# Routed gate and up products with the rows stationary and the weights moving, their result turned by TensorE, and silu in place of tanh of the half

## What is computed

```python
topk_idx, tw = _route(x, router_w, bias)          # 4 of 16 experts for a row
h = jnp.einsum('td,edf->etf', x, gate_w)
u = jnp.einsum('td,edf->etf', x, up_w)
y = jnp.einsum('etf,efd->etd', jax.nn.silu(h) * u, down_w)
routed = jnp.einsum('etd,te->td', y, combine)
sh = jax.nn.silu(x @ sh_gate_w) * (x @ sh_up_w) @ sh_down_w
```

## Time and profile before

| | |
|---|---|
| median of 3 runs | 1787.53 us (1786.2 to 1792.46) |
| the profiled execution's own time | 1785.15 us |
| its span | 1783.4 us |
| mean granted TensorE clock | 0.898 |
| PE busy | 1371.1 us (77%), 11876 matmuls |
| PEld (weight loads) busy | 767.6 us (43%) |
| DVE busy | 1065.8 us (60%) |
| ACT (ScalarE) busy | 1005.3 us (56%) |
| POOL busy | 592.5 us (33%) |

### The profile page before, as it was taken

How to read it: one execution, slowest core, us unless ns; L and a number is a source line. 1 busy time by engine, 2 the same in 40 slices (tenths; PEclk the granted TensorE clock), 3 DMA queues, 4 the chain that set the end, 5 groups by cost and what they waited for, 6 DMA issues and landing times.

```text
span 1783.4 us, 34295 instructions
## 1 busy us (share of the span) xinstructions
PE 1371.1 (77%) x11876; PEld 767.6 (43%) x11876; DVE 1065.8 (60%) x2525; ACT 1005.3 (56%) x1690; POOL 592.5 (33%) x557
## 2 busy tenths in 40 slices
PE   5776476776579898987899989777977785798870
PEld 2211131233225653655356536443545553676650
DVE  7785436454746576477556764874568757234533
ACT  4899577765576698674766976655661121121110
POOL 2100111031533221326332113375535353724426
PEclk9767787898889999998999999988998887999995
DMA  6558400000122342343324323443437423545533
GB/s 191 164 177 197 105 1 24 1 24 13 50 75 66 96 120 54 103 112 107 107 78 111 104 60 96 107 123 117 113 106 202 136 78 94 139 95 142 143 93 118
DMA packets 217939, 180.26 MB, mean 101 GB/s; under 512 B 115467, under 2 KB 188851, under 8 KB 217779
## 3 DMA queue, kind: packets, MB, share of 16 engines
q1 hardware_dynamic: 205491, 144.49, 30.1%
q0 software_dynamic: 12288, 33.57, 6.1%
HBM read 86.25 MB, written 66.58 MB: 86 GB/s over the span
## 4 chain that ended last, share of the span: by engine, by line
PE 37%; ACT 21%; DVE 19%; issue 10%; POOL 7%; DMA 3%; another core or an unknown queue 1%; SPq 1%; POOLq 0%; DVEq 0%; ACTq 0%
ACT big L1131 17%; PE psF L912 8%; DMA big<-in_x 2%; PE psG L762 2%; PE psU L762 2%; PE psY L762 2%; PE psF L762 2%; DVE xc L1462 2%; PE psU L764 2%; PE psF L764 2%; PE psU L763 2%; PE psF L763 2%; POOL big L753 2%; PE psY L763 2%; PE psY L764 2%
## 5 line engine op out<-in xcount | busy, mean ns | idle before, releaser
L1131 ACT ACTIVATE big<-big,text_bias 128x512 f32<-128x512 f32 x1232 | 776.1, 711 | 148.2 <-PE psF L912 59.3
L912 PE MATMUL psF<-big,wslide 128*32 128x512 f32 x2464 | 395.8, 695 | 129.5 <-ACT big L1131 122.0
L698 POOL TENSOR_TENSOR hid_lo<-tile,hid_hi 128x512 f16<-128x512 f32 x128 | 151.0, 1179 | 567.2 <-ACT hid_hi L1146 567.0
L1146 ACT CAST hid_hi<-tile 128x512 f16<-128x512 f32 x128 | 78.4, 613 | 227.8 <-DVE tile L1512 195.4
L762 PE MATMUL psY<-big,hid_hi 128*128 128x256 f16 (+1 forms) x496 | 140.3, 283 | 78.5 <-issue 43.9
L912 PEld LDWEIGHTS psF<-big,wslide 128*32 128x32 f32 x2464 | 54.7, 115 | 290.1 <-ACT big L1131 251.9
L762 PE MATMUL psG<-xg,gate_hi 128*128 128x128 f16 x768 | 159.6, 227 | 11.3 <-issue 4.6
L745 POOL TENSOR_TENSOR work<-work 128x512 f16<-128x512 f32 (+1 forms) x80 | 92.8, 1162 | 219.2 <-DVE work L1636 218.7
L1508 DVE SCALAR_TENSOR_TENSOR tile<-tile,psG 128x512 f32<-128x512 f32 x128 | 87.4, 683 | 123.6 <-ACT tile L1159 108.2
L763 PE MATMUL psG<-xg,gate_hi 128*128 128x128 f16 x768 | 156.1, 222 | 1.4 <-issue 1.4
L764 PE MATMUL psG<-xg,gate_lo 128*128 128x128 f16 x768 | 156.0, 222 | 1.0 <-issue 1.0
(11 more groups left out here) (317 smaller groups left out, 2912.9 us busy)
## 6 DMA issues: line engine op xcount, KB each, us to landing
big<-down_split SPq DMA_DIRECT2D x138, 256.0 KB
y_rows<-tile SPq DMA_DIRECT2D x96, 256.0 KB
xs_rows<-peakT SPq DMA_DIRECT2D x2, 6144.0 KB, 47.6
big<-in_x SPq DMA_DIRECT2D x8, 512.0 KB, 4.5
x<-in_x SPq DMA_DIRECT2D x8, 512.0 KB, 4.0
x_part<-x SPq DMA_DIRECT2D x6, 512.0 KB, 2.6
xc<-x_part SPq DMA_DIRECT2D x24, 128.0 KB
out_x<-xc SPq DMA_DIRECT2D x24, 128.0 KB
```

Source lines behind the costliest of these rows:

```text
L698: pool.tensor_tensor(hid_lo[:, n], tile[:, n], hid_hi[:, n], ALU.subtract).then_inc(glo_done, 1)
L912: last = pe.matmul(psF[32 * j:32 * j + 32, RHO, :], wslide[:, c, 31 - g:63 - g], tanh_tiles[:, n % HRING], start=g == 0 and c == 0, stop=c ...
L1131: act.activation(tanh_tiles[:, n % HRING], feat[:, c], ACT.Tanh, bias=text_bias[:, c, st.batch() * TXT + 4 * g + j:st.batch() * TXT + 4 * ...
L1146: act.copy(hid_hi[:, n], tile[:, n]).then_inc(ghi_done, 1)
```

## The change

- **Products.** Of a routed unit the 128 rows of a block are stationary, and 512 columns of weights (gate and up of the expert, side by side in one array `gu_hi`, `gu_lo`) move: 6 matmuls a block, 12 a unit. The result of a block is one bank with its rows on the partitions. Slot T makes block 0, slot T+1 block 1. Shared units keep their products.
- **Banks.** psG and psU become one tensor of four banks: three go round (unit n has banks 2n mod 3 and 2n+1 mod 3), the fourth, psT, takes the turned result. Block 0 of unit n waits for the product of unit n-2 as before, block 1 for that of unit n-1.
- **Turning.** At T+3 TensorE turns the product, four fp32 transposes into psT (`turn_hidden`); it waits for the product and for the low half of the routed unit before. ScalarE's `hid_hi` moves to T+4 and reads psT; `hid_lo` moves from POOL at T+3 to DVE at T+5 (which stands behind the product of the next unit at its T+2). For shared units both stay.
- **silu.** ScalarE computes `Silu` of the gate part, DVE only multiplies by the up part: one DVE instruction less for each of the 128 units. In a routed unit the Silu waits for both blocks, and where its banks are 2 and 0 (one unit of three) Silu and product are issued as two halves.
- **Registers.** Four expert numbers are packed in a word, so that TensorE and SP load a word for two units; DVE makes the word with two more small instructions for each group.
- **Zero rows.** The two DMAs of 6 MB become 24 of 0.5 MB, one in four slots from slot 2 in steps 1 and 2.
- **Slots.** SOFT moves from 1 to 2 and FILM from 4 to 5.

```diff
-    1, 4, 6, 5, 8, 9, 12, 14, 15, 18, 20, 22, 30, (31, 36), (35, 41), 42, 44, 45, 48, 50)
+    2, 5, 6, 5, 8, 9, 12, 14, 15, 18, 20, 22, 30, (31, 36), (35, 41), 42, 44, 45, 48, 50)
...
+def banks(v):
+
+    return 2 * v.n % 3, (2 * v.n + 1) % 3
+
+
+def bank_freed(v, part):
+
+    return (2 * v.n + part - 3) // 2 + 1
...
+        psE = ctx.enter_context(nc.psum_tensor("psE", [P, 4, 512], F32))
+        psGU, psT = psE[:, 0:3], psE[:, 3]
...
-            zeros = peakT[2 * 32:P, :].unsqueeze(1)
-            for rows in xs_dram:
-                sp.dma_start(rows.rearrange("(n p) c -> p n c", p=P // 2),
-                             zeros.to_broadcast([P // 2, ROWS_G // (P // 2), 2 * D])).then_inc(zero_filled, 16)
+            zeros = peakT[P // 2:P, :].unsqueeze(1).to_broadcast([P // 2, 8, 2 * D])
...
+                if s in (1, 2) and i % 4 == 2 and i // 4 < 12:
+                    cut = xs_dram[s - 1][i // 4 * TOK:(i // 4 + 1) * TOK, :].rearrange("(n p) c -> p n c", p=P // 2)
+                    sp.dma_start(cut, zeros).then_inc(zero_filled[s - 1], 16)
...
                 v = began(T, 3)
-                if v:
+                if v and not v.routed:
                     n = v.n % 4
                     pool.wait_ge(ghi_done, v.n + 1)
...
+            def part(v, p):
+
+                out_ = psGU[:, banks(v)[p]]
                 if v.routed:
-                    for b in range(2):
-                        for f in range(2):
-                            cols = slice((2 * b + f) * P, (2 * b + f + 1) * P)
-                            last = routed_product(ps[:, n, cols], w_hi, w_lo, owners[v.n][b], f, v, b)
+                    e, mine, n = owners[v.r][p], slice(p * P, (p + 1) * P), v.r % XGRING
+                    for k in range(KC):
+                        w_hi, w_lo = (w[:, bass.ds(e, 1), k].rearrange("p o g d -> p (o g d)") for w in (gu_hi, gu_lo))
+                        pe.matmul(out_, xg[:, n, k, mine], w_hi, start=k == 0, stop=False)
+                        pe.matmul(out_, xg[:, n, KC + k, mine], w_hi, start=False, stop=False)
+                        last = pe.matmul(out_, xg[:, n, k, mine], w_lo, start=False, stop=k == KC - 1)
                     return last
...
+            def turn_hidden(v):
+
+                pe.wait_ge(g_done, v.n + 1)
+                if v.kind > 1:
+                    pe.wait_ge(glo_done[1], v.kind - 1)
+                for b in range(2):
+                    for f in range(2):
+                        last = turn(psT[:, (2 * b + f) * P:(2 * b + f + 1) * P], tile[:, v.n % 4, (2 * b + f) * P:(2 * b + f + 1) * P])
+                last.then_inc(turned, 1)
...
+                v = began(T, 3)
+                if v and v.routed:
+                    turn_hidden(v)
...
+                v = began(T, 4)
+                if v and v.routed:
+                    n = v.n % 4
+                    act.wait_ge(turned, v.kind)
+                    act.wait_ge(y_ps, hid_free(UNITS[v.n - 4]))
+                    act.copy(hid_hi[:, n], psT).then_inc(ghi_done, 1)
...
-                    act.activation(tile[:, n], psG[:, v.n % 2], ACT.Tanh, scale=0.5).then_inc(tanh_done, 1)
+                    if v.routed:
+                        act.wait_ge(up_ps, v.n + 1)
+                        for rows, ps in pieces(v):
+                            last = act.activation(rows, ps[:, :, 0:D], ACT.Silu)
+                        last.then_inc(silu_done, 1)
+                    else:
+                        act.wait_ge(gate_ps, v.n + 1)
+                        act.activation(tile[:, n], psGU[:, banks(v)[0]], ACT.Silu).then_inc(silu_done, 1)
...
-                    dve.wait_ge(tanh_done, v.n + 1)
-                    dve.scalar_tensor_tensor(out=tile[:, n], in0=tile[:, n], scalar=1.0, in1=psG[:, v.n % 2],
-                                             op0=ALU.add, op1=ALU.mult).then_inc(v_done, 1)
-                    dve.wait_ge(v_done, v.n + 1)
+                    dve.wait_ge(silu_done, v.n + 1)
                     dve.wait_ge(up_ps, v.n + 1)
-                    dve.tensor_tensor(tile[:, n], tile[:, n], psU[:, v.n % 2], ALU.mult).then_inc(g_done, 1)
+                    blocks = [(rows, ps[:, :, D:2 * D]) for rows, ps in pieces(v)]
+                    for t, u in blocks if v.routed else [(tile[:, n], psGU[:, banks(v)[1]])]:
+                        last = dve.tensor_tensor(t, t, u, ALU.mult)
+                    last.then_inc(g_done, 1)
+                v = began(T, 5)
+                if v and v.routed:
+                    n = v.n % 4
+                    dve.wait_ge(ghi_done, v.n + 1)
+                    dve.tensor_tensor(hid_lo[:, n], psT, hid_hi[:, n], ALU.subtract).then_inc(glo_done[1], 1)
```

More of the change, by code:

```diff
@@ L113 @@
     resident: bool = False
+    kind: int = 0
 def plan():
@@ L148, in plan @@
     stored = [0] * 4
+    kinds = [0, 0]
     for n, v in enumerate(units):
         v.n = n
+        kinds[v.routed] += 1
+        v.kind = kinds[v.routed]
         if v.resident:
@@ L431, in build @@
         front_chain, route_chain = sem("front_chain"), sem("route_chain")
-        gate_ps, up_ps, tanh_done, v_done, g_done, ghi_done, glo_done = (
-            sem(n) for n in ("gate_ps", "up_ps", "tanh_done", "v_done", "g_done", "ghi_done", "glo_done"))
+        gate_ps, up_ps, silu_done, g_done, ghi_done = (
+            sem(n) for n in ("gate_ps", "up_ps", "silu_done", "g_done", "ghi_done"))
+        glo_done = [sem("glo_shared"), sem("glo_routed")]
+        turned = sem("turned")
         y_ps, y_used = sem("y_ps"), sem("y_used")
@@ L486, in gathers, with pieces, both @@
             return gathered[n], 16 * TOPK * (earlier + c // len(comb_rows[g]) + 1)
+        def pieces(v):
+            a, b = banks(v)
+            rows = both(tile[:, v.n % 4])
+            if b == a + 1:
+                return [(rows, psGU[:, a:b + 1])]
+            return [(rows[:, j:j + 1], psGU[:, n:n + 1]) for j, n in enumerate((a, b))]
+        def both(rows):
+            return rows.rearrange("p (b d) -> p b d", b=2)
         def kv_stage(i, sc, st):
@@ L583, in slot @@
                             sp.wait_ge(ids_ready, v.g + 1)
-                        word = sp.value_load(ids[0:1, v.g % 2, v.pair:v.pair + 1])
+                        if v.pair % 2 == 0:
+                            word = sp.value_load(ids[0:1, v.g % 2, v.pair // 2:v.pair // 2 + 1])
+                            owners[v.r] = [sp.snap((word >> (4 * b)) & 15, min_val=0, max_val=E - 1) for b in range(2)]
+                            owners[v.r + 1] = [sp.snap((word >> (4 * b)) & 15, min_val=0, max_val=E - 1) for b in range(2, 4)]
                     for b, n in enumerate(v.entries):
@@ L846, in gate @@
                         pe.wait_ge(ids_ready, v.g + 1)
-                    word = pe.value_load(ids[0:1, v.g % 2, v.pair:v.pair + 1])
-                    owners[v.n] = [pe.snap((word >> (4 * b)) & 15, min_val=0, max_val=E - 1) for b in range(2)]
+                    if v.pair % 2 == 0:
+                        word = pe.value_load(ids[0:1, v.g % 2, v.pair // 2:v.pair // 2 + 1])
+                        owners[v.r] = [pe.snap((word >> (4 * b)) & 15, min_val=0, max_val=E - 1) for b in range(2)]
+                        owners[v.r + 1] = [pe.snap((word >> (4 * b)) & 15, min_val=0, max_val=E - 1) for b in range(2, 4)]
                     pe.wait_ge(xg_loaded[v.r % XGRING], 16 * (v.r // XGRING + 1))
@@ L851, in gate @@
                     pe.wait_ge(lo_ready, Tile(v.tile).at(8, 8))
-                gate_up(v, psG, gate_hi, gate_lo).then_inc(gate_ps, 1)
+                part(v, 0).then_inc(gate_ps, 1)
             def up(v):
-                gate_up(v, psU, up_hi, up_lo).then_inc(up_ps, 1)
+                if bank_freed(v, 1) > 0:
+                    pe.wait_ge(g_done, bank_freed(v, 1))
+                part(v, 1).then_inc(up_ps, 1)
+            def turn_hidden(v):
[6 more added lines that the diff above has]
+                last.then_inc(turned, 1)
             def down_part(v, b):
                 if b == 0:
-                    pe.wait_ge(glo_done, v.n + 1)
+                    pe.wait_ge(glo_done[v.routed], v.kind)
                     if v.y_before:
@@ L1284, in split_expert @@
                 else:
-                    hi, lo = (gate_hi, gate_lo) if what == "gate" else (up_hi, up_lo)
-                    hi, lo, src = hi[:, e], lo[:, e], stage[n % RING].rearrange("p (k d) -> p k d", k=KC)
+                    g = 0 if what == "gate" else 1
+                    hi, lo, src = gu_hi[:, e, :, g], gu_lo[:, e, :, g], stage[n % RING].rearrange("p (k d) -> p k d", k=KC)
                 split(su, hi, lo, src).then_inc(split_done, 1)
@@ L1428, in place @@
                         dve.wait_ge(down_loaded[m % 4], 16 * (m // 4 + 1))
-                two = owner.rearrange("p (w b) -> p w b", b=2)
-                dve.scalar_tensor_tensor(out=ids[0:1, n], in0=two[:, :, 1], scalar=float(E), in1=two[:, :, 0],
+                four = owner.rearrange("p (w b) -> p w b", b=4)
```

(4 more changed lines are left out.)

44 lines of the change are left out of this document (17 added, 27 removed).

## The result

The changed kernel took 1815.12 us (median of 4 runs, 1811.16 to 1818.22), the kernel before beside it 1789.99 us (4 runs): ratio 1.0139, 95% interval 1.0106 to 1.0172. It is slower by 1.4%, and the forecast of 1771 with its range of 1720 to 1808 did not hold it. The profiled execution took 1814.65 us, span 1812.9, 29.5 more than before.

What follows compares the result with a forecast made beforehand. It saw PE and ScalarE nearly full in the scan, latency from 1345 to 1564 us, then PE. Terms -5.6 - 7 - 6 - 8 - 3 - 10 - 2 + 20 + 3 + 2 = -17 gave a median of 1771 us, range 1720 to 1808.

Steps and rivals of the forecast that it cites:

- POOL's low halves: 96 low halves leave POOL's queue: -6 between 1487 and 1564 us, -8 in steps 7 and 8, -3 in 5 and 7.
- rival C: Scan steps, PE and DVE waiting in the new order: they lengthen by what late stretches gain; 1786 us, chance 0.12.
- the same, where chunks are added: Routed products in 20 late units with chunk additions: 5.7 us a unit against 6.04, -7 us, bounds 0 and -20.
- it just fits: Late routed units: 2.2 us from block 1's last column through the low half, against 2.2 us of PE work meanwhile.
- Routed products, late: Last stretch, only units left: 5.0 us a unit against 5.8, 7 units, -5.6 us; bounds 4.9 and 5.5 a unit.
- Zero rows: Step 1: smaller DMAs let the load of x land in time, ending DVE's wait; -10 us, bounds -13 and -5.
- Tables: ScalarE, steps 2 to 8: Silu shares Tanh's table, not Exp's; 49 more loads, +20 us, bounds 0 and +63.
- Scan steps and coupling: Scan steps: added transposes and split Silu and product, +3 us; wait for DVE's product moving to PE, +2 us.
- DVE's first instruction: 32 shared units lose 0.68 us each on DVE where it is not the limit: nothing, down to -5 us.
- SOFT one slot later: ScalarE gets a set of tanh before the Exp that it waits for: -2 us, bounds 0 and -12.
- B: ScalarE, steps 3 to 8: table loads between tanh sets on the path; 1814 us with all 49, chance 0.15.
- The signs that I had named: 50 loads, late units 5.0 us (5.7 with additions), no 1.26 us addition, no in_x wait, step 4 163 to 167.

Runs made afterwards that it cites:

- six fills: Changed kernel with six small chained GpSimd fills for each routed unit, where the kernel before had its low half: 1758.19 us, ratio 0.9875.
- The run with the order changed: Changed kernel with VectorE's low half put ahead of the product: 1771.63 us, ratio 0.9954.
- the run of both: Changed kernel with six GpSimd fills for each routed unit and VectorE's low half ahead of the product: 1732.40 us, ratio 0.9703.

## Why the prediction was wrong, point by point

**The step that failed is "POOL's low halves".** I read in the earlier trace rows that scatters and low halves stand in one queue, and took a relieved POOL for a gain of 6 + 8 + 3 = 17 us. The row was right and the reading of it was not: the low halves were what kept the transfers apart, and I put that at nothing without a reason. Put back as a wait they are worth 31 us, as six fills 43; taken out of the kernel before they cost it part of 58. In place of a gain of 17 stands a loss of 31 to 43 us against the same kernel with the pace kept. The gain itself is not refuted: with the fills the stretch from the last Exp to the first unit of the last group is 18 us shorter than in the kernel before (204.2 against 222.6). How much of that is POOL's relief and how much the shorter products, no run tells apart. The sign was to be had from the trace of before: VectorE's product has this in the view of who waited for whom, on a chip of which one core is in use,

```profile
DVE tile L1512 <- remote: 41.7, 13, 4.1
```

and its long ones lie beside a run of four gathers; ScalarE's wait of 13.9 us, shown above, lies beside rows of 7 and 6 transfers in step 7. I took no row for it and no rival. My rival C, gain lost to order, came nearest in kind, with 15 us.

**The second is "the same, where chunks are added".** I worked out 6.0 us a unit, saw that it was no gain, and then took 5.7 for "the shorter gap of the other unit", with no row under it. Measured: 6.6 and 6.9 in turn, 6.75 in the mean, where before had 5.9 and 6.9, 6.4 in the mean. It was a loss of 0.35 us each where I took a gain of as much. The sequence that I had named, the turning of a unit waiting for the low half of the one before, which stands behind the product, was right; I said of it "it just fits". The run with the order changed prices it at 29 us. The other half of this term held: I took the addition of 1.26 us for the one beside POOL's low half, and with the low halves gone from POOL all 32 of these additions take 0.48 us, where 8 of 32 took 1.26 before.

Routed products, late: predicted 5.0 us a unit against 5.8; measured 5.0. Right, and with the better order 4.4, below my bound of 4.9, so the order cost even there. The bound was wrong too: it counted the gaps of the old down product, 1.86 us, of which the chain of that run has 1.4 a unit.

Zero rows: predicted -10; measured 9.8 in step 1 of the profile and 9 to 12 by the run that undoes it. Right.

Tables: 49 more loads, as counted, and 17 us measured against +20 (13 with the wait). Right in size and place: steps 4 and 6 lose 4.6 us each by them. By the Trainium skill, page "ScalarE: Activation LUTs", section "What ACT_TABLE_LOAD costs", an estimate with its drain of 1380 ns would have made the term about +42; the trace agrees with its 1283 ns and shows no such drain. In the records 44 of the 49 loads begin 17 to 19 ns after the end of the instruction ahead of them, the other five 0.9 to 1.1 us after it, and the next instruction mostly begins 11 or 12 ns after the load's end.

Scan steps and coupling: +3 and +2 predicted. Step 4 went from 162.8 to 166.1 us, within my 163 to 167; with tanh in Silu's place it took 161.5. So without the loads the rest of the change gave 1.3 us there. Step 5 lost 8.3, and with the fills it is back at 188.7, against 188.2 before: that was the pace too.

"DVE's first instruction": nothing, down to -5. This held the change to be neutral where it mattered most. In the late stretch of before the pass lay beside PE, whose matmuls make up nearly all of the chain there; in the new order, where the turning stands behind the product, it would cost 41 us. I costed the removed pass by the old round and not by the new one. SOFT one slot later (-2) was not tried by itself.

Of the rivals, B foretold 1814 for 1815.12, for a wrong reason: it needed 63 us of loads on the path and they cost 17. A right number would not have made the reasons right. The same goes for my own sum: with the pace kept by six fills the change is worth 22 us (ratio 0.9875), near the 17 that I forecast, but with a loss where chunks are added in place of a gain, and with 18 us from the last Exp to the first unit of the last group, more than the 14 that I gave POOL's relief there and in step 7. That it comes out near is in part luck.

The signs that I had named did not warn: 50 loads, late units of 5.0 us, no addition of 1.26 us, no wait for in_x, step 1 at 140.1 us and step 4 at 166.1 all came as said, and none of the three that were to show it wrong came. Only the 5.7 us was off. None of the signs lay in the scatters or the gathers, where the time went.

Left open: by what way POOL's transfers hold TensorE's counts back, and whether it depends on their size. No run here looks below the semaphore records. What is shown is that it was TensorE's counts alone, that they come one after another while the row goes on and together when it ends, and that a stand of 1.1 to 1.2 us or more after each two to five transfers keeps the long holes out of steps 9 and 10. That 29 and 43 us add up to 69 is shown by the run of both.

## What to carry to other kernels

Before you take work from an engine that also issues transfers, look at what the work spaces out: a long row of indirect transfers is a hazard for others, and a small delay in it can be worth many times its length. A wait that ends on "remote" on a single core is no artefact to pass over; follow its semaphore in the timeline. And where a chain is said to "just fit", it decides: order the instruction that frees a bank ahead of the one that fills the next.

## What was not expected of the hardware

TensorE's counts came 14 us late (work done at 1616.60, count at 1630.65) while GpSimd issued 16 indirect gathers in a row, and up to 21 us late behind 19 scatters (1537.21, 1558.32); its clock fell for it. These are the stretches of the changed kernel, columns as in the earlier trace rows:

```profile
1614.00:1620.00 6.00, 5.00 (x33) 2.86 (x31) 1.98 (x3) 0.51 (x1) 4.48 (x6) 1.00 0.87 208
1620.00:1625.00 5.00, 1.49 (x8) 0.51 (x6) 0.00 (x0) 0.00 (x0) 3.78 (x5) 1.00 0.45 128
1625.00:1630.00 5.00, 0.00 (x0) 0.00 (x0) 0.00 (x0) 0.00 (x0) 3.12 (x4) 0.55 0.36 106
1630.00:1636.00 6.00, 1.67 (x8) 1.46 (x9) 1.89 (x3) 1.73 (x3) 0.00 (x0) 0.50 0.29 72
```

PE ended its last matmul at 1621.5 and began the next at 1634.3. The granted clock fell from the full level, 2.4 GHz, to 1.2 GHz at 1625.5 and came back at 1639.1, so that PE worked 4.8 us at half; the hole costs more than its length. It is not the sheer traffic: the 16 DMA engines moved 106 GB/s in the five microseconds in which PE did nothing, while with the six fills they moved 148 GB/s from 1500 to 1560 us and PE was busy for 94% of it. Six fills of 0.15 us between two short rows take away most of the effect, one does not.

A VectorE addition of 128x256 with two operands took 1.26 us beside GpSimd's tensor operation and 0.48 us without it (8 and 24 of the 32 in the late stretch before, all 32 at 0.48 after). Beside the fills it took 0.47 or 0.48 us.

Silu shares its table with Tanh and not with Exp: 25 loads stand ahead of a Silu (L1209, L1213), 24 ahead of an Exp (L1243, L1220), and but for the first one of the program none ahead of a Tanh, though Tanh follows both.
